# GpSimd's sums of x and spikes moved to the last MLP, and the first tiles of the first attention in another order

## What is computed

```python
h = _layernorm(x, axis=-1) * (1 + ca) + sa
x = x + ga * _L0_attn_ref(h, ...)      # a spiking recurrence: 0 or 1 for each token and feature
h = _layernorm(x, axis=-1) * (1 + cb) + sb
x = x + gb * _L0_ffn_ref(h, ...)       # two layers of _layer
...
def _layer(x, wqkv, qs, ksc, wo, lg, lb, w1, b1, w2, b2):
    qkv = shift_token(x) @ wqkv
    q, k, v = ...                       # 8 heads of 64
    q, k = rotary_xpos(l2norm(q) * qs, l2norm(k) * ksc)
    o = local_attention(q, k, v)        # windows of 64, each sees itself and the one before
    x = x + o @ wo
    h = layernorm(shift_token(x)) * lg + lb
    a, g = jnp.split(h @ w1 + b1, 2, axis=-1)
    return x + (a * gelu(g)) @ w2 + b2
```

## Time and profile before

| | us |
|---|---|
| median of 3 runs | 553.61 |
| lowest and highest | 551.92, 554.29 |
| the profiled execution | 551.13 |
| its span in the profile | 549.3 |

### The profile page before, as it was taken

One profiled execution on the slowest core, in us unless ns is written; L12 is line 12 of the kernel. 1 busy time (PEld: TensorE's weight loads), 2 busy tenths in 40 slices (PEclk: granted clock), 3 DMA queues, 4 the chain that ended last, 5 costly groups with the idle time before them and its releaser, 6 DMA issues.

```text
span 549.3 us, 11866 instructions
## 1 busy us (share of the span) xinstructions
PE 491.8 (90%) x4083; PEld 316.1 (58%) x4083; DVE 423.7 (77%) x1173; ACT 351.1 (64%) x1008; POOL 333.1 (61%) x269
## 2 busy tenths in 40 slices
PE   5745087999999998999889999999999999999996
PEld 5425043577777775443466777777544445667775
DVE  6999989799998856566889889995545687566665
ACT  5754017799999986433688999998656526533332
POOL 5980006799999998767998999994110277410000
PEclk9967589999999999999999999999999999999999
DMA  8600002211111112000241111111000000000000
GB/s 306 230 1 2 0 2 51 61 30 41 39 39 33 40 41 68 1 2 0 68 136 31 39 41 39 42 33 38 2 1 0 1 1 1 0 1 21 20 20 19
DMA packets 15184, 21.17 MB, mean 39 GB/s; under 512 B 2410, under 2 KB 9172, under 8 KB 14868
## 3 DMA queue, kind: packets, MB, share of 16 engines
q1 hardware_dynamic: 14836, 20.33, 13.5%
q10 hardware_dynamic: 288, 0.08, 0.1%
HBM read 9.99 MB, written 1.05 MB: 20 GB/s over the span
## 4 chain that ended last, share of the span: by engine, by line
PE 66%; DVE 17%; POOL 5%; issue 5%; ACT 4%; DMA 1%; SPq 0%; DVEq 0%; POOLq 0%; ACTq 0%
PE psT L1564 11%; PE psQK L1658 9%; PE psO L1794 6%; PE psO L1726 5%; PE psQK L2001 5%; PE psS L1774 5%; DVE vst L1147 3%; DVE vAB L1151 3%; PE psS L2073 3%; PE psO L1564 3%; PE psO L2073 2%; PE psQK L1933 2%; ACT lnx L417 2%; POOL rst L756 2%; PE psQK L1808 2%
## 5 line engine op out<-in xcount | busy, mean ns | idle before, releaser
L614 ACT ACTIVATE prob<-psS,nmx 128x128 f32<-128x128 f32 x256 | 90.1, 377 | 18.6 <-DVE nmx L1282 18.6
L936 POOL TENSOR_TENSOR rn<-ssq,half 128x16 f32<-128x16 f32 x30 | 87.3, 2910 | 10.4 <-DVE ssq L1268 10.4
L928 POOL TENSOR_TENSOR ra<-ra,rb 128x512 f32<-128x512 f32 x64 | 82.0, 1300 | 2.5 <-DVE rb L1250 2.2
L756 POOL TENSOR_TENSOR rst<-mv,half 128x4 f32<-128x4 f32 x23 | 24.2, 1054 | 71.3 <-DVE mv L1047 64.0
L1658 PE MATMUL psQK<-wqkv,hsA 128*128 128x512 f32 x128 | 61.4, 596 | 1.2 <-DMA hsA<-z 0.7
L614 ACT ACTIVATION_READ_ACCUMULATOR prob<-psS,nmx 128x1 f32 x256 | 55.2, 216 | 0.0
L944 POOL TENSOR_TENSOR qkn<-ra,rn 128x512 f32<-128x512 f32 x32 | 48.0, 1501 | 5.7 <-ACT rn L532 3.3
L1247 DVE TENSOR_TENSOR ra<-psQK,rope 128x512 f32<-128x512 f32 x64 | 43.9, 685 | 7.5 <-PE psQK L1658 7.0
L1250 DVE TENSOR_TENSOR rb<-psQK,rope 128x512 f32<-128x512 f32 x64 | 43.5, 679 | 0.0
L737 ACT ACTIVATE gel<-psQK 128x512 f32<-128x512 f32 x32 | 19.1, 597 | 37.5 <-PE psQK L2001 37.5
L1261 DVE TENSOR_REDUCE ssq<-sq 128x8 f32<-128x512 f32 x64 | 41.1, 676 | 2.4 <-ACT sq L522 2.2
(11 more groups left out here) (288 smaller groups left out, 1176.7 us busy)
## 6 DMA issues: line engine op xcount, KB each, us to landing
vAB<-vAB SPq DMA_DIRECT2D x62, 128.0 KB, 2.2
wqkv<-in_wqkv SPq DMA_DIRECT2D x2, 768.0 KB, 8.2
big<-in_x SPq DMA_DIRECT2D x4, 256.0 KB, 4.8
ra<-in_rope_t SPq DMA_DIRECT2D x1, 1024.0 KB, 7.2
ropeb<-in_rope SPq DMA_DIRECT2D x1, 1024.0 KB, 8.6
big<-in_ew SPq DMA_DIRECT2D x2, 512.0 KB, 6.3
wmod<-in_wmod SPq DMA_DIRECT2D x2, 384.0 KB, 6.7
out<-big SPq DMA_DIRECT2D x3, 256.0 KB, 2.3
```

Of the source, the lines that this page charges most:

```text
L614: act.activation(prob[:, k, :], psS[:, hb, c * P:(c + 1) * P], ACT.Exp, bias=nmx[:, k:k + 1], accum_out=sums[:, n % 2, k:k + 1]).then_inc( ...
L928: pool.tensor_tensor(o, o, rb[:, r], ALU.add).then_inc(s["sum_" + name], 1)
L936: pool.tensor_tensor(rn[:, :], ssq[:, :], half[:, :], ALU.pow).then_inc(s["rn_ready"], 1)
```

## The change

Four things move. GpSimd's four sums into x_cm go from the beginning of the first MLP to the second layer's MLP, behind the second layer-norm scales. The two loads of the experts' weights, which wait for these sums, go from SP's work ahead of the second layer's attention to behind its last V halves. On ScalarE the squares of q of tile 0 go ahead of the output z of group 1. And in the first layer's steps -2 and -1 every engine's order is another: q and k of tile 0 are turned ahead of the product of V, the three fillers between them are gone, the projections of q and k of tile 2 stand behind the scores of tile 0, and the copies, exponentials, maxima and z outputs are ordered to match. Nothing is computed in another way.

```diff
--- before.py
+++ after.py
@@ -375,14 +375,13 @@
                     sp.wait_ge(s["ln_out"], ln_no(1, 0) + 1)
                     sp.dma_start(hsA[0:64, P:GW], z[0:64, P:GW]).then_inc(s["hsA_dma0"], 16)
                     sp.dma_start(hsA[64:128, P + 1:GW + 1], z[64:128, P:GW]).then_inc(s["hsA_dma0"], 16)
-                else:
-                    sp.wait_ge(s["x_mixed"], NG)
-                    sp.dma_start(ew1, a["ew1"]).then_inc(s["ld_ew"], 16)
-                    sp.dma_start(ew2, a["ew2"]).then_inc(s["ld_ew"], 16)
                 for g in ((1, 2, 3) if l == 0 else (3,)):
                     stack_in(l, g)
                 for i in range(NT):
                     v_halves(l, i)
+            sp.wait_ge(s["x_mixed"], NG)
+            sp.dma_start(ew1, a["ew1"]).then_inc(s["ld_ew"], 16)
+            sp.dma_start(ew2, a["ew2"]).then_inc(s["ld_ew"], 16)
 
             outr = out.rearrange("b t d -> (b t) d").rearrange("(n p) d -> p n d", p=P)
             for g in range(NG - 1):
@@ -562,8 +561,8 @@
             ln_norm(ln_no(1, 1))
             squares_k(0)
             ln_norm(ln_no(1, 2))
+            squares_q(0)
             stack_out(1)
-            squares_q(0)
             norms(0)
             ln_norm(ln_no(1, 3))
 
@@ -630,27 +629,36 @@
                     mlp_ln_out(l, 0)
                     act.wait_ge(s["table"], GELU_AFTER[l])
                     load_table(ACT.Gelu)
-                if n == 2 - LEAD:
+                if n == 1 - LEAD:
+                    squares_k(1)
+                    q_turned(0)
+                    k_turned(0)
+                    squares_q(1)
+                    v_copy(0)
+                    stack_out(NG - 2)
+                    norms(1)
+                elif n == 2 - LEAD:
+                    exps(0, 0)
+                    exps(0, 1)
                     stack_out(NG - 1)
-                if has(i + 3) and i > -LEAD:
-                    squares_k(n + 3)
-                    if n == 1 - LEAD:
-                        stack_out(NG - 2)
-                    if i != 2 - LEAD:
+                    squares_k(2)
+                    squares_q(2)
+                    q_turned(1)
+                    k_turned(1)
+                    v_copy(1)
+                else:
+                    if has(i + 3) and i > -LEAD:
+                        squares_k(n + 3)
+                        if i != 2 - LEAD:
+                            squares_q(n + 3)
+                    if has(i + 1):
+                        exps(n + 1, 0)
+                        exps(n + 1, 1)
+                    if i == 2 - LEAD:
                         squares_q(n + 3)
-                if n == 1 - LEAD:
-                    v_copy(0)
-                if has(i + 1):
-                    exps(n + 1, 0)
-                    exps(n + 1, 1)
-                if i == 2 - LEAD:
-                    squares_q(n + 3)
-                if has(i + 2):
-                    q_turned(n + 2)
-                    k_turned(n + 2)
-                    if n == 1 - LEAD:
-                        norms(1)
-                    if n != 1 - LEAD:
+                    if has(i + 2):
+                        q_turned(n + 2)
+                        k_turned(n + 2)
                         v_copy(n + 2)
                 if has(i):
                     o_turned(n)
@@ -961,9 +969,6 @@
                 for i in range(-LEAD, NT):
                     attention(l, i)
                 if l == 0:
-                    pool.wait_ge(s["spikes"], 2)
-                    for g in range(NG):
-                        pool.tensor_tensor(x_cm[:, gsl(g)], x_cm[:, gsl(g)], spikes[:, gsl(g)], ALU.add).then_inc(s["x_mixed"], 1)
                     phase_scalars()
                     phase_whole()
                 ln_rstd(ln_no(2 + l, 0))
@@ -975,6 +980,10 @@
                     pool.wait_ge(s["rope_q"], 2 * NT)
                     pool.wait_ge(s["ld_wa"], 64)
                     rope_tables(1)
+                else:
+                    pool.wait_ge(s["spikes"], 2)
+                    for g in range(NG):
+                        pool.tensor_tensor(x_cm[:, gsl(g)], x_cm[:, gsl(g)], spikes[:, gsl(g)], ALU.add).then_inc(s["x_mixed"], 1)
                 ln_rstd(ln_no(2 + l, 2))
                 if l == 0:
                     phase_sine()
@@ -1344,15 +1353,18 @@
 
                 n = l * NT + i
                 early = i == 1 - LEAD
-                if i == 2 - LEAD:
+                if n == 2 - LEAD:
+                    negmax(0, 0)
+                    negmax(0, 1)
+                    q_normed(1)
+                    rope_products(2, 1)
+                    rope_products(2, 0)
+                elif i == 2 - LEAD:
                     rope_products(n + 3, 1)
                     negmax(n + 1, 0)
                     negmax(n + 1, 1)
-                    if l:
-                        q_normed(n + 2)
+                    q_normed(n + 2)
                     rope_products(n + 3, 0)
-                    if l == 0:
-                        q_normed(n + 2)
                 elif has(i + 3) and i > -LEAD and not early:
                     rope_products(n + 3, 1)
                     rope_products(n + 3, 0)
@@ -1841,16 +1853,15 @@
                 if has(i):
                     weigh_v(l, i)
                 if n == 1 - LEAD:
+                    turn_qk(0, 0)
                     proj_v(0, 0)
-                    proj_part(0, 2, 1)
-                    keep_clock(3, psT1[:, :])
-                    turn_qk(0, 0)
-                    proj_part(0, 2, 0)
                 elif early:
                     turn_qk(l, 0)
                     proj_v(l, 0)
                 elif has(i + 2):
                     if n == 2 - LEAD:
+                        proj_part(0, 2, 1)
+                        proj_part(0, 2, 0)
                         ln_t2(ln_no(1, NG - 1))
                     proj_v(l, i + 2)
                     if n == 2 - LEAD:
```

## The result

The median after the change is **544.85 us** (544.79 to 545.27 in four runs) against 553.47 us before (551.92 to 554.29): a ratio of 0.9849, with a 95% interval of 0.9827 to 0.9871. The direction and most of the mechanisms were right; the size was not. The profiled execution after took 544.79 us (span 543.0) against 551.13 before, so the profiles differ by 6.3 us and the medians by 8.6.

What follows compares the result with a forecast made beforehand. TensorE alone was taken to bound the attention loop, while in the first MLP ScalarE waits for GpSimd's scales. Terms 1.7 + 2.8 + 0 + 0.9 = 5.4 us off the median 553.6 gave 548.2 us, range 546.2 to 551.4.

Steps and rivals of the forecast that it cites:

- I set the forecast on the median: Final step: 5.4 us subtracted from the three runs' median of 553.6, not from the profiled execution of 551.13, giving 548.2.
- part 4: Second attention's start: expert weights' transfers moved behind V's halves, removing TensorE's 1.56 us wait; 0.9 us, bounds 0.1 and 1.56.
- The 6.4 us landing: Second attention's start, before the change: a V transfer takes up to 6.4 us to land behind the weights.
- Part 1: Start of the first attention, new order: 1.7 us gained, bounds 0.7 and 2.0.
- The start: First attention's run on TensorE begins at 91.95 in place of 92.22: 0.27 us won.
- The three fillers: First attention's start: three fillers vanish from TensorE, 0.81 us recorded, about 0.7 counted.
- the gap of 0.18 us before a projection: First attention's start: TensorE's gap while ScalarE's squares stood behind its exponentials closes, counted as 0.18 us.
- The head start: First attention's loop, limited by TensorE: the gain lasts to its end; rival that neither loop keeps it: 550.8, chance 0.12.
- Part 2: GpSimd's sums out of the first MLP: 1.64 us to the first product plus 1.14 to the second group's, 2.8 together.
- The collision: First MLP, VectorE's copy against GpSimd's phase product on shared ports; rival that it returns: 1.64 for 2.8, 549.4, chance 0.13.
- Part 3: Sums in the last MLP end 0.8 us before the residual that waits for them: cost 0, bound 0.5.
- The slower one: First attention's start: without the three fillers TensorE's clock falls to the lower level, 559.8 us; chance 0.03.

Runs made afterwards that it cites:

- ew_last: Kernel before with only the expert weights' transfers moved behind the last V halves: median 550.20 us against 553.34, ratio 0.9951.
- before_third: Kernel before, unchanged, traced a third time: an ordinary execution of 553.75 us.
- nmx_first: Changed kernel with VectorE's two maxima of tile 1 ahead of the scaling of q of tile 2 in the second attention's step 0: 545.22 us.
- before_again: Kernel before, unchanged, traced a second time: an execution of 551.26 us.
- fill_mlp: Kernel before with six TensorE fillers ahead of the first MLP's first layer-norm turn: 555.01 us against 553.23, ratio 1.0028.
- fill_v_wait: Kernel before with six TensorE fillers ahead of the second layer's first wait for V's halves: 552.35 us against 553.97, ratio 0.9971.
- fill_second: Kernel before with eight TensorE fillers ahead of the turn of q and k of the second layer's second tile: 553.97 us against 553.23, ratio 1.0007.

## Why the prediction was wrong, point by point

- **The step that failed: "I set the forecast on the median."** The terms were read from one execution, in which V's wait was 1.56 us, and subtracted from a median 2.5 us above it, as if part 4 took away no more than that execution showed. By medians part 4 is 3.1 us (ew_last), not 0.9: 2.2 of the 3.35 us by which the forecast missed. What it takes away beyond the profile shows in one ordinary execution of before (before_third): a product with V 1.2 us later and, behind the longer wait, 1.7 us of lower clock. The fillers that kept the clock up there were worth 1.6 us by medians. That the whole excess lies there isn't shown, since the new order alone also took more off the median (3.4 us) than off its profile (2.2). Set against the profiled execution, the same sum gives 545.7, within 0.9 us of the result. The three runs shown spread over 2.4 us, and the forecast did not ask which stage could spread so. The 6.4 us landing beside a median of 2.8 was the hint: a wait on such a transfer is no fixed price.
- **Part 4 in the profile itself** was 1.21 for 0.9, inside its bounds. Without the wait the turn of the output did become the next limit, as said: it waits 0.47 us for VectorE at 277.76 in the changed kernel.
- **Part 1 was under-sized: 2.43 for 1.7**, and above its upper bound; as the last step it is 2.8 by medians, which is 1.1 more of the miss. The start is little at fault: the first attention's run starts at 92.16 to 93.20 in eight traces with the old order (mean 92.43, or 92.32 without the last of them) and at 91.78 to 92.30 in five with the new (92.07), so 0.25 to 0.36 us for 0.27 (0.44 in the pair of traces that gave the 2.43). The three fillers gave 94.66 - 94.01 = 0.65 for 0.7. The term that was mis-sized most is the gap of 0.18 us before a projection. From start to start, the projection's two halves took 1.21 + 0.93 us before and 1.71 together after, so 0.43. The bracket showed only the idle part; around it, the group ahead of the gap no longer overlaps with the one behind it, and that one has a record of 1.10 us where the same two products take 1.02 without a gap. For the turn of tile 0's output the forecast had counted this (0.46 + 0.2, measured 7.94 - 7.26 = 0.68), for the projection it had not. Another 0.17 us lay between the eight fillers and the next turn (1.90 us from start to start before, 1.73 after) in no bracket at all. The head start lasted through the loop, as forecast: from its third step to the last but one, a step takes 7.25 us in both orders.
- **Part 2 held in both halves:** 10.70 - 9.06 = 1.64 as forecast, and 9.85 - 8.76 = 1.09 for 1.14. The collision moved to copies that nobody waits for: at 213.33 VectorE's copy takes 0.91 us beside GpSimd's product (211.59 to 213.95), and 0.42 us at 218.48 alone. That is what the Trainium skill (SBUF — State Buffer, SBUF: two separate sides) says of the two engines' shared ports: whoever comes second is held up. This trace agrees: the copy ended at 214.24, 0.29 us behind the product. The last phase product ended at 217.70, 0.8 us ahead of the copy; the margin was forecast at 1.1.
- **Part 3 held:** the sums end 0.90 us ahead of the residual (0.8 forecast).
- **The rivals.** None of them was the case, and none stood on the side of a larger gain. The slower one had the size wrong and the place nearly right: just ahead of the start the granted clock did fall in one of the five traces with the new order (nmx_first), which cost some 0.5 us and not 11.6, since from 92 us on it is 1.00 again. The old order, meanwhile, was paying for the clock at 282 us in before_third. The profile of before, with 1.00 from 75 us on, did not show it; its other traces did.

## What to carry to other kernels

When the runs of a kernel spread more than their profile explains, find the wait that can vary, a transfer that is released late and lands late, before sizing a change: what removes it is worth its mean, not what one trace shows, and a forecast against the traced execution is then the better of the two (here 545.7, against 548.2 from the median, with 544.85 measured). Transfers that are needed much later don't belong ahead of one that an engine waits for, even where the one trace shows the wait at a microsecond. And size a closed gap on TensorE from start to start of the groups around it, since the bracket leaves out the overlap that is lost with it.

## What was not expected of the hardware

- The granted clock fell in executions of one and the same kernel in different gaps: 0.57 after a wait of 1.88 us at 274.3 (before_again), 0.68 after 2.60 us at 282.2 (before_third); in the first trace of before, with 1.88 and 1.56 us at these places, it stayed at 1.00. The two levels are 1.2 and 2.4 GHz; a projection of V took 1.97 us in the window at 0.68 and 1.13 at 1.00.
- It fell ahead of the first attention too, in three of the thirteen traces (fill_mlp, fill_v_wait, nmx_first: 0.57, 0.59 and 0.64 from 88 to 92 us), behind waits of about 1.30 and 0.70 us that stand there in all thirteen. A projection took 2.00 to 2.07 us there in place of 1.13.
- The issue of one and the same transfer (L367, 128 KB) took SP 0.43 or 0.44 us in five traces and 1.25 to 1.94 in eight, and everything behind it on SP moved with it. The cause isn't known. In the changed kernel it took 1.25 us and did no harm, since V's first half then lands 2 us before it is needed. A late issue doesn't settle the landing either: with the weights ahead, V's first half took 5.3 to 7.3 us to land in seven traces, and in fill_second, where the issue took 1.94 us, the product with V waited 1.66 us only.
- Ahead of the first attention the executions differ by up to 0.9 us (the first turn of probabilities at 104.00 to 104.95 in eight traces with the old order), so a term under half a microsecond can't be read from one pair of traces there.
